# Two experts to a round, W1 in 64-column halves, and a new order of the stages

## The reference, cut to what matters

```
x = x + conv_block(ln_c(x))      # x: 4 x 64 x 64 x 16
t = tokens(x)                    # rows of 64 features
t = t + ffn(ln_t(t))

conv_block:  2-D DCT; window attention on 8x8 blocks (q, k normed, softmax over 16x16, 4 heads), projection;
             beside it gelu(1x1 conv), gelu(depthwise 3x3), + x_dct, gelu(1x1 conv), + ; mixed with coef; inverse DCT
ffn:         probs = softmax(t @ Wr + br); top 2 of 8 experts, weights renormed to sum 1
             xn = layernorm(t)
             h_e = gelu((xn * ln_g[e] + ln_b[e]) @ W1[e] + b1[e])     # 64 -> 256
             y_e = h_e @ W2[e] + b2[e]                                # 256 -> 64
             out = sum over the two chosen experts of weight * y_e
```

## Time and profile before

| | us |
|---|---|
| median of 3 runs (260.77 to 261.13) | 260.94 |
| the profiled execution | 260.44 |
| its span, first to last instruction | 258.4 |
| TensorE matmul busy | 228.3 (88%) |
| TensorE weight load busy | 117.9 (46%) |
| DVE busy | 151.1 (58%) |
| ACT busy | 129.8 (50%) |
| POOL busy | 47.0 (18%) |

### The profile page before, as it was taken

How to read it: one execution, slowest core, us unless ns; L and a number is a source line. 1 busy time by engine, 2 the same in 40 slices (tenths; PEclk the granted TensorE clock), 3 DMA queues, 4 the chain that set the end, 5 groups by cost and what they waited for, 6 DMA issues and landing times.

```text
span 258.4 us, 3162 instructions
## 1 busy us (share of the span) xinstructions
PE 228.3 (88%) x1206; PEld 117.9 (46%) x1206; DVE 151.1 (58%) x266; ACT 129.8 (50%) x206; POOL 47.0 (18%) x44
## 2 busy tenths in 40 slices
PE   2857699999996967978479999999999999999993
PEld 2744589848462655977333223223223332333230
DVE  0791849999797798777993424424424433443344
ACT  1246741003508064166447566567567666766670
POOL 3850095003562048003300000000000000000000
PEclk9995999999997999999759999999999999999999
DMA  6970000000000000000009315080511707062001
GB/s 232 256 196 0 3 0 4 0 0 0 3 0 1 0 0 3 0 0 3 0 22 232 85 44 128 0 203 3 134 28 42 164 0 164 0 143 63 0 0 41
DMA packets 6590, 14.18 MB, mean 55 GB/s; under 512 B 2736, under 2 KB 4144, under 8 KB 5680
## 3 DMA queue, kind: packets, MB, share of 16 engines
q1 hardware_dynamic: 6576, 13.99, 22.0%
HBM read 12.81 MB, written 1.18 MB: 54 GB/s over the span
## 4 chain that ended last, share of the span: by engine, by line
PE 79%; DVE 12%; ACT 6%; DMA 1%; issue 1%; SPq 0%; DVEq 0%
PE psum L623 24%; PE psum L638 23%; PE psum L482 6%; PE psum L454 3%; PE psum L464 3%; PE psum L422 2%; DVE place L985 2%; ACT place L673 2%; PE psum L570 2%; ACT place L667 2%; PE psum L552 2%; PE psum L395 1%; PE psum L536 1%; PE psum L445 1%; PE psum L490 1%; PE psum L561 1%
## 5 line engine op out<-in xcount | busy, mean ns | idle before, releaser
L780 ACT ACTIVATE hid<-psum,b1p 128x512 f32<-128x512 f32 x128 | 77.8, 688 | 40.5 <-PE psum L623 40.5
L1075 DVE SCALAR_TENSOR_TENSOR term<-psum,sm,wide 128x512 f32<-128x512 f32 x32 | 24.0, 751 | 71.8 <-PE psum L638 71.8
L623 PE MATMUL psum<-tok,w1s 128*128 128x512 f16 x256 | 64.8, 390 | 0.0
L638 PE MATMUL psum<-hid,w 128*64 128x512 f32 x256 | 61.8, 604 | 0.0
L623 PEld LDWEIGHTS psum<-tok,w1s 128*128 128x128 f16 x256 | 22.0, 100 | 51.4 <-ACT hid L780 27.4
L638 PEld LDWEIGHTS psum<-hid,w 128*64 128x64 f32 x256 | 15.6, 136 | 32.0 <-issue 27.0
L1080 DVE TENSOR_TENSOR x<-x,term 128x512 f32<-128x512 f32 x32 | 22.2, 692 | 1.1
L482 PE MATMUL psum<-h_pad,tap_bd 128*128 128x512 f32 x36 | 15.8, 592 | 0.0
L395 PE MATMUL psum<-c,xs 128*128 128x128 f32 x32 | 7.6, 431 | 5.6 <-DMA xs<-in_x 5.6
L907 DVE SCALAR_TENSOR_TENSOR place<-h_pad,sm,place 128x512 f32<-128x512 f32 x16 | 12.0, 752 | 0.6
L482 PEld LDWEIGHTS psum<-h_pad,tap_bd 128*128 128x128 f32 x36 | 6.7, 189 | 8.2 <-issue 8.2
(11 more groups left out here) (135 smaller groups left out, 293.4 us busy)
## 6 DMA issues: line engine op xcount, KB each, us to landing
wide<-gate_store SPq DMA_DIRECT2D x14, 512.0 KB, 6.3
xs<-in_x SPq DMA_DIRECT2D x2, 512.0 KB, 5.1
w1f<-in_W SPq DMA_DIRECT2D x2, 512.0 KB, 9.6
block_out<-x SPq DMA_DIRECT2D x4, 256.0 KB, 6.5
wide<-gate_store SPq DMA_DIRECT2D x2, 384.0 KB, 5.0
hid<-in_W1T SPq DMA_DIRECT2D x1, 512.0 KB, 10.4
w<-in_W SPq DMA_DIRECT2D x1, 512.0 KB, 12.0
c<-const SPq DMA_DIRECT2D x1, 483.5 KB, 4.2
```

What stands on the lines that cost most here:

```text
L623: mm = pe.matmul(h_bank(n), w1s[:, part, e, k * P:(k + 1) * P], tok[:, pair, half, b, :], start=part == 0, stop=part == 1)
L638: mm = pe.matmul(y_bank(u)[b * H:(b + 1) * H, :], w2[:, e * KT + k, :], hid[:, u % 2, B2 * k + b, :], start=k == 0, stop=k == KT - 1)
L780: act.activation(hid[:, u % 2, t, :], h_bank(n), ACT.Gelu, bias=b1p[:, e * KT + k:e * KT + k + 1]).then_inc(gelu_ready, 1)
L1075: dve.scalar_tensor_tensor(term[:, u % 2, :], y_bank(u), b2t[:, e:e + 1], gate_b[part][:, e % (E // 2), :], ALU.add, ALU.mult).then_inc(te ...
```

## The change

It has four parts.

1. Units come in rounds of two. In round r TensorE does down(2r), down(2r + 1), up(2r + 4), up(2r + 5); rounds -2 and -1 are up(0) to up(3) alone. W1 is four units ahead in place of one. `hid` gets two more buffers, laid over `w1f` and `w1g`, which are free once `w1s` is made.
2. Each W1 matmul of 128 columns is cut in two of 64 columns, written to partitions 0 to 63 and 64 to 127 of the same bank, with the same moving tokens.
3. PSUM: two h banks in units 0 to 3 and six after; two y banks from the start. So the gates of both pairs must have left slot(p, 0) early: W2 of unit 1 and W1 of unit 4 wait for the gate rows of both pairs. `shares` of pair 1 gets turn 29 (before 111), `gates_to_rows` and `keep_gates` 91 and 101 (before 45 or 36, and 141).
4. The other turns are new too. On a few stages pair 1 comes earlier or later against pair 0; `biases` goes from turn 10 to turn 3 on DVE.

```
-    "windows": (4, 8), "conv_in": (5, 9), "keep_dw": (3, 6), "keep_xd": (4, 7), "gelu_in": (5, 9),
+    "windows": (4, 7), "conv_in": (6, 9), "keep_dw": (3, 5), "keep_xd": (4, 7), "gelu_in": (6, 8),
...
+ROUNDS = UNITS // 2
+AHEAD = 2
+def round_turn(r):
+    return 100 + 10 * (r + 1)
...
-        h_early = [bank(slot(0, 1), 0), bank(slot(0, 1), 1), bank(slot(0, 0), 1)]
-        h_late = h_early + [bank(slot(1, 1), 0), bank(slot(1, 1), 1)]
-        y_early = [bank(slot(0, 0), 0)]
-        y_late = y_early + [bank(slot(1, 0), 0)]
+        h_early = [bank(slot(0, 1), 0), bank(slot(0, 1), 1)]
+        h_late = h_early + [bank(slot(1, 1), 0), bank(slot(1, 1), 1), bank(slot(1, 0), 1), bank(slot(0, 0), 0)]
+        y_banks = [bank(slot(0, 0), 1), bank(slot(1, 0), 0)]
-        EARLY = UNITS // PAIRS
+        EARLY = 2 * AHEAD
...
+        hid_of = [hid[:, 0], hid[:, 1]] + [w[:, :, :].rearrange("p (t a) n -> p t (a n)", t=TILES) for w in (w1f, w1g)]
...
                     for part in range(2):
-                        mm = pe.matmul(h_bank(n), w1s[:, part, e, k * P:(k + 1) * P], tok[:, pair, half, b, :],
-                                       start=part == 0, stop=part == 1)
+                        for side in range(2):
+                            mm = pe.matmul(h_bank(n)[side * H:(side + 1) * H, :],
+                                           w1s[:, part, e, k * P + side * H:k * P + (side + 1) * H], tok[:, pair, half, b, :],
+                                           start=part == 0, stop=part == 1)
...
-                if u == 0:
-                    pe.wait_ge(gates_ready, 1)
+                if u == 1:
+                    pe.wait_ge(gates_ready, PAIRS)
...
-            def experts(u):
-                if u + 1 < UNITS:
-                    up(u + 1)
-                if u >= 0:
-                    down(u)
+            def experts(r):
+                if r >= 0:
+                    down(2 * r)
+                    down(2 * r + 1)
+                for u in (2 * (r + AHEAD), 2 * (r + AHEAD) + 1):
+                    if u < UNITS:
+                        up(u)
...
+            def gelu_hidden(u):
                 e = u % E
-                if u > 1:
-                    act.wait_ge(w2_done, u - 1)
+                if u > 3:
+                    act.wait_ge(w2_done, u - 3)
```

## The result

| | before | changed |
|---|---|---|
| median of the runs made together | 260.97 us (4 runs, 260.77 to 261.13) | 250.70 us (4 runs, 248.42 to 252.42) |
| ratio, 95% interval | | 0.958 (0.950 to 0.966) |
| the profiled execution | 260.44 us | 248.42 us |
| its span | 258.4 us | 246.4 us |

The forecast was 249.0 us with a range of 246.0 to 253.0: the direction and the size hold. But its parts do not all hold: the gain of the new stage order, 4.4 us in the sum, does not show where the order is changed alone, and other terms made up for it. The ratio leaves out executions over 1.5% above the fastest of the same kernel, since these can be in a slower state of the chip. The executions of the changed kernel lie 4 us apart, more than the four of the kernel before in that job; later jobs had the kernel before at 257.5 to 263.9 us.

A forecast was written before the change was run, and what follows sets the result against it. The prediction took TensorE to bound the expert loop, 47% of the span. Terms of -4.4, -2.0, +8.1 and -13.7 us made -12.0 from 260.94, so 248.9, forecast 249.0 us, range 246.0 to 253.0.

The forecast's parts named there:

- the new stage order: Reordered stages ahead of the expert loop, up to tokens(1): -4.4 us in the sum.
- The cost of a change between W1 and W2: Expert loop on TensorE: 0.10 us into W2, 0.15 us back, from matmul shape; gone when both are 64 columns wide.
- A unit of 3.45 us: Expert loop: W1 at 1.73 plus W2 at 1.72 us per unit, against 3.70 to 3.85 before.
- First W1 to first W2: Start of the loop, four W1 units ahead with two h banks: 13.8 us where before 5.7, so +8.1 us.
- The rest of the loop: From the first W2 on: 32 W2 and 28 W1 units in 103.5 us instead of 116.9, -13.7 us.
- low(1): Between 87 and 119 us: moved behind inverse_over_kw(0), it no longer covers TensorE's wait for keep_back(0), +1.6 us.
- rival (b): Ahead of the loop: the new stage order gives nothing, other waits take its place; +4.4 us, 253.4; chance 0.13.
- the front: Stages up to gram_matrices, which starts at 32.7 instead of 35.58 us: -2.9 us, bounds 0 to -4.3.
- the middle: Stages from 35 to 87 us: less TensorE idle and no low clock at times_wv(0), -3.1 us, bounds 0 to -4.
- the 116: Ahead of the loop: tokens(1) expected at 113 us; later than 116 us would make the prediction wrong.
- rival (a): Expert loop: half of the switches stay because the cost is the f16/f32 change; +4 us, 253; chance 0.10.
- The clock rival: Start of the loop: TensorE's gaps with two banks keep the clock low for four W1 units; +2.9 us, 252; chance 0.08.

The follow-up runs named there:

- unit 0 early: The changed kernel with W1 of unit 0 moved ahead of features(1) and its gelus, two and two, ahead of high_part(1) and keep_tokens(1): 247.82 us, ratio 0.952.
- POOL later: The changed kernel with POOL's weights_of_first waiting for first_taps(0) instead of keep_xt(0): 249.90 us, ratio 0.965.
- low(1) back: The changed kernel with low(1) back ahead of inverse_over_kh(0) and residual(0) behind mix_branches(1), as before the change: 249.10 us, ratio 0.962.

## Why the prediction was right, and where it was not

**Right in its main mechanism.** The cost of a change between W1 and W2 is one of shape, not of type: the transpose's rows said so, and the whole-column run and the halves-only run confirm it (7.14 against 6.88 us a round; 3.45 a late unit). A unit of 3.45 us was measured at 3.44. The halves' weight loads are hidden. The Trainium skill, TensorE: Matmul & The Clock Gate, Part 3, says that a load overlaps running matmuls only where the row group differs; that sentence does not hold for these column halves, which share their rows and keep 0.216 us a pair, as W2's cadence had let expect. (The same part of the Trainium skill also lets loads run ahead into a background weight buffer, which the prediction did not weigh.) First W1 to first W2: 13.8 us expected, 12.4 measured, with 0.70 to 0.71 us a tile at the full clock where 0.72 was worked out, transposes of 0.26 us each where 0.7 stood for two, and none of the 0.5 us for small ACT steps. The rest of the loop: 103.2 us expected, 242.48 - 138.96 = 103.5 measured. low(1): +1.6 expected, +1.83 measured. A slip without effect: 77.8 / 128 is 0.608 us a gelu, not 0.605.

**Wrong: the stage order, -4.4 us.** That was rival (b), given 0.13, with the right place; it looked for the new waits between DVE and ACT, and the one that was found is between POOL and DVE. Measured, the order alone is worth about nothing (1.001, 0.996 to 1.005); with the rounds the traces agree, and the medians leave it open. Three terms failed.

First, the front, -2.9: at a like clock it is worth 1.36 us. I worked out that a faster ACT brings keep_xt(0) forward, and did not ask what waits for it. POOL's W1 product does, and it meets first_taps(0) on DVE: 5.43 us instead of 3.77 behind it, so that 0.46 us of the front is left.

Second, the middle was to bring 3.1 us and brought 1.27 at the full clock, which is what the sum has without its 1.8 for the low clock of times_wv(0). That low stretch is in two of the three traces with the old order and in none of the eleven with the new one. But in three of the six traces where low(1) is moved, the clock falls in or just behind the wait that the move lays bare, ahead of inverse_over_kh(0), which then takes 3.44 to 3.78 us instead of 2.05 (the new order alone, unit 0 early, POOL later), and in none of the five with low(1) back. So the falls may go with the waits, and the new order may trade one for another; no run isolates this.

Third, the clock in the first 35 us is not fixed by the order: the two traces of the changed kernel differ by 2.1 us there. In the second of them tokens(1) comes at 116.23 us, later than the 116 that the prediction named as a sign of being wrong.

**The sum came out by luck.** The profiled execution has 246.4 us of span, exactly the 258.4 - 12.0 of the forecast, but its parts differ from the terms. tokens(1) came 3.3 us earlier (-4.4 in the sum), and of these 3.3 a part is the clock: before, it was low from 19.9 to 26.7 us and from 81.3 to 84.7, and here ahead of tokens(1) only from 11.2 to 14.6. From tokens(1) to the first W1 it was -2.1 (-2.0), from there to the first W2 +6.8 (+8.1), and the rest -13.4 (-13.7). The start of the loop was put 1.3 us too dear and made up for the order, 1.1 too good. The medians have -10.3.

**What was attributed to the wrong part.** The sum gave rounds, banks and halves together -7.6 us from the router's end on; in the profiled executions it was 115.9 - 124.6 = -8.7. The halves alone have -7.2 (245.63 - 128.29 = 117.3), the rounds and buffers 1.5: the transpose's wait of 2.1 us is gone, and from the first W1 on they cost 0.7 (115.9 against 115.2). The prediction did not part these. Its rival (a) took the f16/f32 change for the cost, so that halves would win nothing and rounds half of the switches; without the rounds, 31 changes of shape each way had to go by the halves alone, and they did.

**The clock rival.** (c) did not occur: the clock came back 4.0 us after the first W1 (126.55 to 130.6). Its premise, a gap behind each second tile, did not arise either: TensorE was busy without a gap until then, and the gaps of 0.2 us came with the full clock. What let it fall is only partly known: a 3.6 us idle is not needed, gaps of 0.3 to 0.8 us with the 8-column router matmuls between them were enough, and with these filled it did not fall there.

## What to carry to other kernels

Where two matmul streams alternate on TensorE, give them one shape before reordering them: cutting a 128-column f16 matmul in two 64-column halves cost nothing here and removed 0.25 us of each alternation. When a stage is moved forward, list everything that waits on its signal, also on engines that are not the bound: POOL's start was such a one, and took back 0.9 of the 1.36 us that the front won. Compare a reordering between the same two instructions over several traces, at a like clock, and against the kernel before in the same job: the clock falls in other places from trace to trace, and a fall behind a wait costs 1.6 us and more.

## What the runs showed of the hardware

- Two 64-column f16 matmuls of 512 on the halves of one PSUM bank take 0.216 us a pair, as one of 128 columns, loads included, though a 64-column f16 load takes 0.111 us in the record against 0.100 for 128 columns.
- Going from a 128-column matmul to a 64-column one costs 0.10 us here and the way back 0.15 (7.14 against 6.88 us a round), and the next weight load starts no earlier than its matmul; at one width, f16 and f32 alternate with no cost that the rows show (3.45 + 3.43 us a round).
- A DVE step with two SBUF operands took 4.16 us instead of 0.76 beside a POOL product of 128x2048, and 2.26 beside a POOL cast; DVE products with one operand in PSUM were not held up (1.15 us).
- The granted clock fell at 121.8 us with no idle stretch over 0.8 us since 111.64, and it differs from run to run in the first third of the kernel: 16.96 against 18.75 us for the same instructions. This makes a part of the spread of some 4 us between executions of one kernel; not all, since two executions with a mean clock of 0.979 took 248.31 and 250.93 us.
